# Flamingo block on one core: first attention without key and value work, group 0 routed beside group 2, paired score banks and stationary probabilities in the second attention

## The reference

```
x = x + tanh(g_xattn[0]) * L0_xattn(layernorm(x), ctx)   # one head: softmax((xW'+b) ctx') ctx
x = x + tanh(g_ffn[0])   * L0_ffn(layernorm(x))          # 16 experts, top 4 of sigmoid scores, + a shared one
x = x + tanh(g_xattn[1]) * L1_xattn(layernorm(x), ctx)   # 16 heads of 8: q, k, v, softmax, output matrix
x = x + tanh(g_ffn[1])   * L1_ffn(layernorm(x))          # 8 experts, top 2 of softmax, silu(gate)*up
```

## Time and profile before

| | us |
|---|---|
| runs without the profile | 336.18, 337.23, 338.31 (median 337.23) |
| the profiled execution, its whole time | 339.97 |
| span in that execution (what the rows below add up to) | 337.3 |
| stage A with its loads, to the first down matmul of B | 0 to 56.8 |
| stage B | 56.8 to about 146 |
| stage C | about 146 to 257.8 |
| stage D, with the store | 257.8 to 337.3 |

### The profile page before, as it was taken

How to read it: one execution, slowest core, us unless ns; L and a number is a source line. 1 busy time by engine, 2 the same in 40 slices (tenths; PEclk the granted TensorE clock), 3 DMA queues, 4 the chain that set the end, 5 groups by cost and what they waited for, 6 DMA issues and landing times.

```text
span 337.3 us, 5717 instructions
## 1 busy us (share of the span) xinstructions
PE 296.4 (88%) x1488; PEld 222.8 (66%) x1488; DVE 247.9 (73%) x727; ACT 165.1 (49%) x427; POOL 103.8 (31%) x157
## 2 busy tenths in 40 slices
PE   1889879998998999858898898898887999999995
PEld 1677756665766666537787787787874667676662
DVE  2479778976887977654868868868868877958662
ACT  1237653224233242466798797797862233233321
POOL 6216615020055010263529829829401010100000
PEclk9999958999899999987999999999999999999999
DMA  7901104818605125000000000000004233061550
GB/s 216 328 16 38 31 4 153 247 28 256 166 26 176 54 97 157 0 1 0 2 1 3 2 0 0 0 0 1 3 17 154 83 121 116 22 209 36 165 179 31
DMA packets 16279, 26.45 MB, mean 78 GB/s; under 512 B 2789, under 2 KB 5299, under 8 KB 16051
## 3 DMA queue, kind: packets, MB, share of 16 engines
q1 hardware_dynamic: 15448, 24.93, 24.0%
q10 hardware_dynamic: 808, 1.25, 1.3%
HBM read 24.29 MB, written 1.25 MB: 76 GB/s over the span
## 4 chain that ended last, share of the span: by engine, by line
PE 54%; DVE 17%; ACT 8%; DMA 7%; issue 6%; SPq 3%; POOL 2%; DVEq 1%; ACTq 0%; POOLq 0%
PE bank L547 20%; PE Ybank L569 13%; DMA CR<-comb_rows 4%; PE bank L722 4%; ACT PX L977 3%; DVE cmx L1327 2%; DVE xn L1088 2%; PE Tb L471 2%; DMA comb_rows<-ct 2%; DVE st L1074 2%; SPq L295 1%; DMA CB<-in_consts 1%; DVE recT L1343 1%; SPq L302 1%; DVE xl L1094 1%
## 5 line engine op out<-in xcount | busy, mean ns | idle before, releaser
L890 ACT ACTIVATE sg<-bank 128x512 f32<-128x512 f32 x64 | 38.1, 597 | 76.6 <-PE bank L547 59.4
L334 POOL TENSOR_TENSOR rstd<-ve,mhalf 128x4 f32<-128x4 f32 x16 | 16.2, 1011 | 162.2 <-DVE ve L1081 162.2
L1227 DVE TENSOR_TENSOR hb<-sg,CR 128x512 f32<-128x512 f32 x64 | 44.9, 703 | 18.4 <-DMA CR<-comb_rows 8.4
L1220 DVE TENSOR_TENSOR sg<-sg,bank 128x512 f32<-128x512 f32 x64 | 43.5, 680 | 6.7 <-PE bank L547 4.2
L1327 DVE TENSOR_REDUCE cmx<-bank 128x4 f32<-128x308 f32 x64 | 28.3, 472 | 17.5 <-PE bank L695 17.2
L342 POOL TENSOR_TENSOR KS<-kr,CB 128x1232 fp32r<-128x1232 f32 x16 | 36.1, 2260 | 11.3 <-PE bank L695 11.3
L547 PE MATMUL bank<-xh,WBH 128*128 128x512 f32 x68 | 36.2, 533 | 1.2 <-DVE sg L1220 0.6
L547 PE MATMUL bank<-xh,UPH 128*128 128x512 f32 x64 | 36.2, 566 | 0.0
L569 PE MATMUL Ybank<-hb,W2T 128*128 128x512 f32 x64 | 33.5, 604 | 3.1 <-DVE hb L1227 3.1
L569 PE MATMUL Ybank<-hb,downw 128*128 128x512 f32 x64 | 33.0, 599 | 0.4 <-DVE hb L1227 0.3
L977 ACT ACTIVATE PX<-bank,cmx 128x77 f32<-128x77 f32 x128 | 29.4, 355 | 0.0
(11 more groups left out here) (179 smaller groups left out, 612.0 us busy)
## 6 DMA issues: line engine op xcount, KB each, us to landing
CR<-comb_rows SPq DMA_DIRECT2D x64, 128.0 KB, 3.0
CR<-comb_rows SPq DMA_DIRECT2D x32, 256.0 KB, 3.4
VX<-in_vs_seed SPq DMA_DIRECT2D x4, 320.0 KB, 4.6
w13raw<-in_w SPq DMA_DIRECT2D x1, 1088.0 KB, 11.6
X<-in_x SPq DMA_DIRECT2D x4, 256.0 KB, 9.5
upraw<-in_up SPq DMA_DIRECT2D x4, 256.0 KB, 4.7
out_x<-X SPq DMA_DIRECT2D x4, 256.0 KB, 3.6
cT<-in_ctxT SPq DMA_DIRECT2D x4, 154.0 KB, 6.1
```

Source lines behind the costliest of these rows:

```text
L334: nc.gpsimd.tensor_tensor(rstd[:], ve[:], mhalf[:], ALU.pow).then_inc(rstd_rdy, 1)
L890: A(sg[:, k % 2, :], Gb[k % 2][:], ACT.Silu).then_inc(m.s_done, 1)
L1220: V.tensor_tensor(sg[:, k % 2, :], sg[:, k % 2, :], Ub[k % 2][:], ALU.mult).then_inc(m.t2, 1)
L1227: V.tensor_tensor(hb[:, k % 2, :], sg[:, k % 2, :], CR[:, k % RING, :], ALU.mult).then_inc(m.h_done, 1)
```

## The change

In words:

- Stage A has no key or value work any more. Values and keys are projected after the last mix of A and around the first two units of B. ACT writes the values with room for a ninth column per head (`HV = 9`, the ones of the sum), with no bias: the bias goes through the output matrix once (`bv_mm`) and into the row that is added to x anyway. Keys are split by ACT and DVE straight from the projection. Their repetition down the partitions is now 16 DMAs of SP (`place_keys`), and the values take 24 (`place_values`), two for a unit of B from unit 10 on. The four loads of vs_seed and the 24 early scatters are gone.
- The loop of A is written out. ACT applies the norm of groups 2, 3 and of group 0 for B. The exponentials of A give their sums themselves (`accum_out`), in place of a DVE sum. The order is turned so that scores run two groups ahead, and the routing of B's group 0 stands beside group 2.
- The routing weights go to DRAM with one DMA in place of four.
- In C the score banks are two pairs. Maxima, subtraction and exponentials are one instruction for each pair (616 wide), for all four quads the same way. `pt` is double-buffered. The mix has `pt` as the stationary operand and the value columns (18 or 27) as the moving one, after one matmul that writes zeros. The sums come out as one column per head. DVE inverts 128x16 and multiplies once, a new transpose (`c_turn`) and a new ACT copy (`c_turned`) bring the result to the output matrix. POOL places no values.
- D is as before, except for the single write of the weights.

The core of the difference:

```diff
             def later_load(n):
-                if n < 4:
-                    ... VX ... vs_seed
-                elif n < 8: ... upraw
-                elif n < 10: ... downw
+                if n < 4: ... upraw
+                elif n < 6: ... downw
+                first, per = 6, 2
...
+                for i in range(per * (n - first), per * (n - first) + per):
+                    if 0 <= i < NHG * 4:
+                        place_keys(i)
+                    elif 0 <= i - NHG * 4 < len(pieces):
+                        place_values(i - NHG * 4)
+            def place_keys(n):
+                a, s = n // NHG, n % NHG
+                src = kh if a < 2 else kl
+                sp.dma_start(kr[32 * a:32 * (a + 1), s, :], src[32 * s:32 * (s + 1), :].bitcast(F32)).then_inc(in_kr, 16)
...
-                for t in range(GB):
-                    sp.dma_start(at[0:m.E, t * P:(t + 1) * P], ct[32 * t:32 * t + m.E, :]).then_inc(rows_out, 16)
+                sp.dma_start(at[0:m.E, :].rearrange("e (t n) -> t e n", t=GB), ct[0:GB * m.E, :]).then_inc(rows_out, 16)
```

```diff
-            def c_mix(g, t, u, first):
+            def c_mix(g, t, first):
...
-                for c in range(u * CU, (u + 1) * CU):
-                    w = chunk_rows(c)
-                    v = (t % 2 * NC + c) * P
-                    i = mm(bOut[t % 2][:, u * P:(u + 1) * P], VX[0:w, v:v + P], pt[0:w, c * P:(c + 1) * P],
-                           start=c % CU == 0, stop=c % CU == CU - 1)
+                pe.wait_ge(c_fin, START + n)
+                mm(bO9, RQ[:, 0, 1:5, :].rearrange("p a b -> p (a b)"), ZR[:], start=True, stop=False,
+                   skip_group_check=True)
+                pe.wait_ge(c_ev, START + 3 * n + 3)
+                for c in range(NC):
+                    w, m = chunk_rows(c), chunk_heads(c)
+                    h = c // CU * UH + chunk_head(c)
+                    v = VS[0:w, c, 0:m, bass.ds(n, 1), :].rearrange("p i a d -> p i (a d)")
+                    i = mm(bO9[:, h * HV:(h + m) * HV], pt[0:w, t % 2, c * P:(c + 1) * P], v, start=False,
+                           stop=c == NC - 1, skip_group_check=True)
...
-            def c_exps(g, t, s, first=False):
+            def c_exps(g, t, u):
                 n = GB * g + t
+                act.wait_ge(c_sub, START + NU * n + u + 1)
+                p = PX[:, t % 2, u * UK:(u + 1) * UK]
+                A(p, p, ACT.Exp).then_inc(c_exp, 1)
...
             def c_normalize(g, t):
                 n = GB * g + t
-                dve.wait_ge(c_rs, START + n + 1)
-                dve.wait_ge(c_wo, START + n)
-                V.tensor_tensor(OTs[0:UD, :], bOut[t % 2][0:UD, 0:P], recT[0:UD, :], ALU.mult)
-                V.tensor_tensor(OTs[UD:P, :], bOut[t % 2][UD:P, P:2 * P], recT[UD:P, :],
+                mixed = bO9.rearrange("p (h d) -> p h d", h=NH)
+                dve.wait_ge(c_pv, START + n + 1)
+                V.reciprocal(rec[:], mixed[:, :, HD]).then_inc(c_rs, 1)
+                dve.wait_ge(c_rs, n + 1)
+                dve.wait_ge(c_ot, START + n)
+                V.tensor_tensor(On[:], mixed[:, :, 0:HD], rec[:].unsqueeze(2).to_broadcast([P, NH, HD]),
                                 ALU.mult).then_inc(c_norm, 1)
```

More of the change, by code:

```diff
@@ L818, in _ @@
             A = nc.scalar.activation
[L819 removed]
+            for s in (a_ptc, c_ev, c_otc, mB.y_cp, mD.y_cp):
                 act.sem_inc(s, START)
@@ L1035, in _ @@
             m_y_copy(m, NG - 1)
-            for s in range(NHG):
-                c_exps(0, 0, s, first=True)
+            for u in range(NU):
+                c_exps(0, 0, u)
             c_body(0, True, False)
```

784 lines of the change are left out of this document (397 added, 387 removed).

## The result

The changed kernel takes 362.6 us (358.2 to 365.5, four runs) where the kernel before takes 336.8 (336.2 to 338.3): 7.2% slower, ratio 1.072, 95% interval 1.061 to 1.082. The forecast was 316. The profiled execution took 365.5, a span of 363.7.

What follows compares the result with a forecast made beforehand. The prediction found no engine full in C, a chain through all setting 6.4 us a tile. Savings of 9 (A), 3 (B), 8.5 (C) and 0.5 (D), 21 from 337.3, gave 316.3, taken as 316; range 306 to 328.

Steps and rivals of the forecast that it cites:

- comparison with the present loop at full clock: In C, the argument against a cold-clock rival (chance 0.05, up to 356 us): the present loop idles PE as much.
- A loop's period: In C, a tile's loop was put at 5.8 us, a group at 24.2 in place of 25.5.

## What to carry to other kernels

A matmul with few moving columns fills PE's record but, in these runs, not its clock: before a mix is turned so that it moves fewer columns, ask what it saves (here next to nothing, 2.35 us for twenty against 2.44 to 2.54 with five times the columns) and count what the clock may cost, with a cold tile's price. A comparison with the present loop at full clock has to hold both equal, the idle time and the columns moved beside it. When work is taken off one stage, follow it to where it lands on every engine: GpSimd's expansions made VectorE's work on SBUF longer in each of three places (by 2.3, 1.95 and 3.9 us). A loop's period must be made for each tile with its extra work, not for the plain one. And before a stage's length in one profile is laid to an edit, look whether the clock fell in it: the same group of B took 24.0 to 24.8 us without a fall and 25.6 to 27.4 with one.
